# Cross attention scores: one float32r product of 96 stacked rows in place of a float32 product of 32 rows

## The chip, the cores and the metric

The program runs on one core of one Trainium2 chip. The metric is the device time of one execution in microseconds, the median of the runs shown. Lower is better. The core's engines are TensorE (PE, with its weight loads as PEld), VectorE (DVE), ScalarE (ACT), GpSimd (POOL) and SyncE (SP, which here only issues DMAs).

## The reference, cut to what matters

Six layers are applied to x (8 batches of 128 tokens, width 128) one after another, each with a residual: self attention, a cross attention to a context of 77 rows per batch, a mixture of 16 experts, a second self attention, the second cross attention, a mixture of 8 experts. The change touches only the two cross attentions:

```python
q = (query @ Wq + bq).reshape(B, Nq, H, D).transpose(0, 2, 1, 3)      # H = 16 heads, D = 8
k = (key_value @ Wk + bk).reshape(B, Nkv, H, D).transpose(0, 2, 1, 3) # Nkv = 77
v = (key_value @ Wv + bv).reshape(B, Nkv, H, D).transpose(0, 2, 1, 3)
attn = jnp.einsum('bhqd,bhkd->bhqk', q, k) * scale
attn = jnp.clip(attn, -CLAMP, CLAMP)          # the first cross attention only
attn = jax.nn.softmax(attn, axis=-1)
x = jnp.einsum('bhqk,bhkd->bqhd', attn, v).reshape(B, Nq, Cq)
return x @ Wo + bo
```

## The kernel before

The program is a row of blocks, written by hand, one instruction stream per engine, with semaphores between them; all engines meet between two blocks. In order: `setup_and_bias` (loads, keys and values of both cross attentions), `attention0` (the first self attention, four rounds; beside it GpSimd and SyncE prepare operands of later layers), a layer norm, `cross_attention(0)`, `mixture0`, `attention1`, a layer norm, `cross_attention(1)`, the rest of `mixture1`, `store`.

**Preparation beside attention0.** GpSimd makes `kblk` (L594): for each layer and batch a 128 x 308 tile, whose columns are 4 heads of a group times 77 keys. A row of head j holds the keys of that head in the columns of j and zeros elsewhere, so that one product of the 32 rows of a group of four heads gives the scores of all four. Behind that GpSimd splits the weights of 17 experts (L607, L609) that SyncE loads into two buffers (L584).

**cross_attention(l).** The queries of all 1024 tokens are two products of 512 columns (L666) that ScalarE moves to `q` with the bias (L740). Then there are 16 steps n, two for each batch; a step is 8 heads. In a step: the scores of two groups of four heads (L688, two products, in two banks of `x_score`); VectorE reads them (in layer 0 a clamp to `x_s`, L782, then the maximum, L799; in layer 1 the maximum, L785, then the subtraction, L803); GpSimd subtracts the maximum in layer 0 (L829); ScalarE takes the exponential (`x_p`, L769); TensorE transposes the 8 heads (`x_turn`, L722); ScalarE moves them to `x_pT` (L764); TensorE multiplies by the values (`x_pv`, L712). Once per batch the result is turned back (`x_back`, L732), normalized (L814, L818), turned again (L695) and multiplied by Wo (L680), added to x (L790), and the next layer norm is made (L795 to L837, L701).

TensorE's stream is software pipelined: in iteration n it issues the Wo product of an older batch, the scores of step n, the small turns, the values product of step n-2, the turn of step n-1 and the turn back. This order is fixed in the code:

```python
for u in range(2):
    at = 32 * (2 * (n % 2) + u)
    mm = pe.matmul(sbk[n % 2][:, u, 0:HG * NKV], q[at:at + 32, P * b:P * b + P],
                   kblk[l][at:at + 32, b, :], start=True, stop=True)
mm.then_inc(S["scores_done"], 1)
```

In layer 1 SyncE has one thing to do in this block: at its start it issues the first loads of the last mixture (`loads`); in layer 0 it has nothing.

Of the kernel before, what the change touches and what calls it, by code (L numbers as in the profile page):

```python
# [21 lines left out]
P = 128  # L22
B = 8
# [19 lines left out]
HG = 4  # L43
# [48 lines left out]
def program(nc, a, out, scratch, spread0):  # L92
# [30 lines left out]
    kblk = [sb(f"kblk{l}", [P, B, HG * NKV]) for l in range(2)]  # L123
# [98 lines left out]
    def setup_and_bias(bias0, w0):  # L222

        wq, wkv, wo = w0
        with ExitStack() as st:
            sb, ps, sem = tools(st, "su_")
# [107 lines left out]
    def attention0(bias0, w0):  # L334
# [3 lines left out]
        with ExitStack() as st:  # L338
# [15 lines left out]
            one = sb("one", [P, 1])  # L354
            fb = [ps(f"fill{j}") for j in range(2)]
# [5 lines left out]
                     "oT_dve", "y_done", "y_free", "kblk_done", "ld", "cast", "one_set", "landed0", "landed1")  # L361
            S = {n: sem(n) for n in names}
            block = st.enter_context(nc.Block())
# [210 lines left out]
            def _(sp):  # L574
# [6 lines left out]
                for e in range(E0 + 1):  # L581
                    if e >= 2:
                        sp.wait_ge(we_split, 2 * (e - 1))
                    sp.dma_start(raw[e % 2][:, :], a["experts0"][e].rearrange("p k m -> p (k m)")).then_inc(  # L584
                        S[f"landed{e % 2}"], 16)
                sp.wait_ge(S["ld"], 80)

            @block.gpsimd
            def _(pool):
                pool.memset(one[:, :], 1.0).then_inc(S["one_set"], 1)  # L590

                for l in range(2):
# [10 lines left out]
                pool.wait_ge(S["one_set"], 1)  # L603
# [7 lines left out]

    def cross_attention(l, loads=None):
# [3 lines left out]
        SLOTS = B + 2  # L616
        bo = (bo_x0, bo_x1)[l]
        with ExitStack() as st:
            sb, ps, sem = tools(st, f"x{l}_")
            q = sb("q", [P, T])  # L620
# [17 lines left out]
                     "xT_out", "pv_zeroed")  # L638
            if not xsem:
                xsem.update({n: gsem("x_" + n) for n in names})  # L640
            S = xsem
            one_layer = {"q_done": 2, "q_out": 2, "with_bias": 1, "pv_zeroed": 1, "slot_done": SLOTS}
            one_layer |= {n: STEPS for n in ("scores_done", "scores_read", "max_done", "shifted", "exp_done",
                                             "turn_done", "turned_out", "pv_done")}
            since = {n: l * one_layer.get(n, B) for n in names}
# [12 lines left out]
            if loads is not None:  # L658
# [1169 lines left out]
```

## Time and profile before

| | |
|---|---|
| median of 3 runs | 656.82 us (656.3, 656.82, 679.62) |
| span of the profiled execution (its own time beside the span isn't given) | 631.4 us |
| median less span | 25.4 us |
| busy in the span | PE 533.0, PEld 413.8, DVE 374.3, ACT 326.1, POOL 206.7 us |
| mean granted TensorE clock | 0.884 |
| window 190 to 262 us (cross attention 0) | PE 57.24 of 72 us, granted clock 0.83 |
| window 455 to 525 us (cross attention 1 from its scores on, and the start of mixture 1) | PE 60.66 of 70 us, granted clock 0.77 |
| the groups of L688 (scores) | 128 instructions, 28.5 us busy |

The table is read from the outside in: the span and the work around it make the time, the busy shares say which engine is nearest to the limit, and the windows say in which stage the changed lines lie. A share of busy time is no waiting time: which wait ends last in a step is seen only in the timeline of that step. The granted clock is the share of 2.4 GHz: 1.00 is 2.4 GHz and 0.50 is 1.2 GHz.

### The profile page before, as it was taken

Reading aid. Unit: us, or ns where it says so; the run is one execution under the profiler, and the core shown is the slowest. Engines: PE = TensorE matmul, PEld = TensorE weight load, DVE = VectorE, ACT = ScalarE, POOL = GpSimd, SP = SyncE. Lnnn points to the kernel's source line nnn. Section 1 sums busy time; section 2 is a strip of 40 time slices with the busy share of each in tenths; the row PEclk is TensorE's granted clock in tenths of the full one; section 3 lists DMA queues with packets and bytes.
Section 4 is the critical chain, followed back from the end, with each engine's and each line's share of the span. In section 5 each row is a group of like instructions: output and inputs, shape, how many; then the busy total and the mean of one; then the engine's idle time right before and its main releaser. Section 6 shows DMA issues by size and latency. Waiting matters only on the chain. (4 is left out here: it accounts for less than half of the span.)

```text
span 631.4 us, 9987 instructions
## 1 busy us (share of the span) xinstructions
PE 533.0 (84%) x3281; PEld 413.8 (66%) x3281; DVE 374.3 (59%) x875; ACT 326.1 (52%) x573; POOL 206.7 (33%) x229
## 2 busy tenths in 40 slices
PE   4698999989866998589999699864499967999996
PEld 2488898978853665457887387724266645777774
DVE  3376584756643465356666417765536638788875
ACT  3265454645403566435555326530246636788893
POOL 1688600000013346216655173011200255445510
PEclk9899999999876699789999569978559978899998
DMA  6913100000000000024432100000200001111201
GB/s 182 214 56 88 50 0 0 0 0 1 1 0 1 1 2 1 1 84 134 135 120 66 50 2 2 0 1 1 67 1 1 3 1 34 33 35 42 59 0 33
DMA packets 23412, 23.71 MB, mean 38 GB/s; under 512 B 3358, under 2 KB 17648, under 8 KB 23152
## 3 DMA queue, kind: packets, MB, share of 16 engines
q1 hardware_dynamic: 22528, 22.66, 12.5%
q10 hardware_dynamic: 848, 0.60, 0.3%
q8 instruction: 20, 0.33, 0.2%
q14 instruction: 16, 0.13, 0.1%
HBM read 22.64 MB, written 0.61 MB: 37 GB/s over the span
## 5 line engine op out<-in xcount | busy, mean ns | idle before, releaser
L1775 DVE TENSOR_TENSOR e_h_lo<-e_h,e_h_hi 128x512 fp32r<-128x512 f32 x60 | 50.7, 875 | 15.5 <-ACT e_h_hi L1636 15.4
L1045 POOL TENSOR_TENSOR e_gc<-e_g,e_c 128x512 f32<-128x512 f32 x32 | 42.0, 1314 | 42.0 <-ACT e_g L1028 22.4
L180 POOL TENSOR_TENSOR rstd<-var,eps_pow 128x4 f32<-128x4 f32 x8 | 8.3, 1039 | 134.0 <-DVE var L170 133.9
L722 PE MATMUL x_turn<-consts,x_p 128*77 128x128 f32 x256 | 42.3, 317 | 9.3 <-ACT x_p L769 9.3
L764 ACT ACTIVATE x_pT<-x_turn 77x1024 f32<-77x1024 f32 x32 | 32.6, 1020 | 32.9 <-PE x_turn L722 32.9
L1632 ACT ACTIVATE e_h<-e_h,m_b 128x512 f32<-128x512 f32 x64 | 43.6, 688 | 10.2 <-PE e_h L1534 10.2
L722 PEld LDWEIGHTS x_turn<-consts,x_p 128*77 128x77 f32 x256 | 33.7, 172 | 19.2 <-ACT x_p L769 16.4
L1093 DVE TENSOR_TENSOR e_h_lo<-e_h,e_h_hi 128x512 fp32r<-128x512 f32 x34 | 23.8, 699 | 26.0 <-ACT e_h_hi L1004 26.0
L1004 ACT ACTIVATE e_h_hi<-e_h 128x512 fp32r<-128x512 f32 x34 | 21.5, 632 | 33.9 <-DVE e_h L1087 28.2
L1636 ACT ACTIVATE e_h_hi<-e_h 128x512 fp32r<-128x512 f32 x64 | 38.6, 633 | 0.0
L416 PE MATMUL a_score<-a_kT,a_qz 128*128 128x128 f32 x256 | 34.5, 278 | 2.8 <-DMA rows<-in_L_xattn_bo 2.8
L416 PEld LDWEIGHTS a_score<-a_kT,a_qz 128*128 128x128 f32 x256 | 32.5, 192 | 4.2 <-issue 3.2
L444 PE MATMUL a_pv<-a_v,a_pT 128*128 128x65 f32 x256 | 33.6, 277 | 0.0
L485 ACT ACTIVATE a_qz<-a_fill 64x512 f32<-64x512 f32 x32 | 18.9, 591 | 28.1 <-PE a_fill L395 25.8
L444 PEld LDWEIGHTS a_pv<-a_v,a_pT 128*128 128x128 f32 x256 | 33.2, 201 | 0.3
L546 DVE SCALAR_TENSOR_TENSOR a_s<-a_score,w_bias 128x512 f32<-128x512 f32 x32 | 22.1, 690 | 18.0 <-PE a_score L416 17.7
L1674 POOL TENSOR_TENSOR m_w_hi<-m_w,e_one 128x512 fp32r<-128x512 f32 x16 | 17.5, 1096 | 44.7 <-PE e_y L1534 29.0
L829 POOL TENSOR_TENSOR x_s<-x_s,x_m 128x616 f32<-128x616 f32 x16 | 19.5, 1216 | 31.7 <-DVE x_m L799 31.7
L688 PE MATMUL x_score<-kblk,x_q 32*128 32x308 f32 x128 | 28.5, 561 | 1.6 <-ACT x_q L740 1.6
L515 ACT ACTIVATE a_p<-a_s 128x512 f32<-128x512 f32 x32 | 20.1, 629 | 18.2 <-DVE a_s L552 18.2
L782 DVE TENSOR_SCALAR x_s<-x_score 128x616 f32<-128x616 f32 x16 | 12.8, 799 | 27.2 <-PE x_score L688 26.7
L834 POOL TENSOR_TENSOR rstd<-var,eps_pow 128x1 f32<-128x1 f32 x16 | 9.0, 562 | 58.1 <-DVE var L809 58.1
(275 smaller groups left out, 1448.6 us busy)
## 6 DMA issues: line engine op xcount, KB each, us to landing
e_c<-spread SPq DMA_DIRECT2D x32, 256.0 KB, 3.2
m_w<-in_L_ffn_W SPq DMA_DIRECT2D x16, 256.0 KB, 3.0
a_raw<-in_experts SPq DMA_DIRECT2D x17, 192.0 KB, 2.4
su_reversed<-scratch SPq DMA_DIRECT2D x1, 1024.0 KB, 6.3
w_wkv<-in_L_attn_Wkv SPq DMA_DIRECT2D x1, 1024.0 KB, 8.7
a_pick_f<-in_pick SPq DMA_DIRECT2D x1, 768.0 KB
x_all<-in_x SPq DMA_DIRECT2D x1, 512.0 KB, 5.6
w_wq<-in_L_attn_Wq SPq DMA_DIRECT2D x1, 512.0 KB, 6.6
```

What stands on the lines that cost most here:

```text
L416: mm = pe.matmul(sbk[n % 2][:, h, :], qz[:, hg % 2, h, P * b:P * b + P], kT[:, hg % 2, h // 2, P * b:P * b + P], start=True, stop=True)
L444: mm = pe.matmul(ob[g % 2][:, h, 0:DH0 + 1], pT[g % 2][:, h, :], v[:, hg % 2, b, h, :], start=True, stop=True)
L546: dve.scalar_tensor_tensor(out=s[k][:, :, :], in0=sbk[k][:, :, :], scalar=SC, in1=bias0[:, NG * hg:NG * hg + NG, :], op0=ALU.mult, op1=ALU ...
L688: mm = pe.matmul(sbk[n % 2][:, u, 0:HG * NKV], q[at:at + 32, P * b:P * b + P], kblk[l][at:at + 32, b, :], start=True, stop=True)
L722: mm = pe.transpose(tb[0:NKV, u, P * j:P * j + P], p[k % 2][:, u, j, :], ident)
L764: act.activation(pT[k % 2][:, :, :], tb[0:NKV, :, :], ACT.Copy).then_inc(S["turned_out"], 1)
L1004: act.activation(h_hi[u % 2][:, :], h[u % 2][:, :], ACT.Copy).then_inc(S["hi_done"], 1)
L1045: pool.tensor_tensor(gc[k % 2][:, :], g[u % 2][:, :], c[k % NC][:, :], ALU.mult).then_inc(S["weighted"], 1)
L1093: dve.tensor_tensor(h_lo[u % 2][:, :], h[u % 2][:, :], h_hi[u % 2][:, :].bitcast(F32), ALU.subtract).then_inc(S["lo_done"], 1)
L1632: act.activation(h[half][f], hb[f][:, :], ACT.Gelu, bias=b1[j][:, f:f + 1]).then_inc(S["gelu_done"], 1)
L1636: act.activation(h_hi[half][f - 1][:, :], h[half][f - 1], ACT.Copy).then_inc(S["hi_done"], 1)
L1775: dve.tensor_tensor(h_lo[half][f][:, :], h[half][f], h_hi[half][f][:, :].bitcast(F32), ALU.subtract).then_inc(S["lo_done"], 1)
```

## The change

The scores are made of operands split in two float32r parts, high and low: q = q_hi + q_lo, k = k_hi + k_lo. Three of the four partial products are kept, stacked along the contraction: rows 0 to 31 hold q_hi against k_hi, rows 32 to 63 q_hi against k_lo, rows 64 to 95 q_lo against k_hi. So a group of four heads takes one float32r product of 96 rows and 308 columns in place of a float32 product of 32 rows.

The stacked keys (`kstack`) lie in DRAM, written beside `attention0`, and are loaded batch by batch into four buffers `ks`. The stacked queries `qs` are made in each cross attention by 24 copies from SBUF to SBUF, since each group's 32 rows must come to partitions 0, 32 and 64. The semaphores of `setup_and_bias` are cleared and freed at the start of `attention0` to have enough of them.

```diff
@@ attention0, GpSimd
-                    for b in range(B):
-                        pool.tensor_tensor(kblk[l][:, b, :].rearrange("p (h k) -> p h k", h=HG),
-                                           free(ctx_kT[l][:, b, :], [[0, HG], [1, NKV]]),
-                                           free(head_in_group, [[1, HG], [0, NKV]]),
-                                           ALU.mult).then_inc(S["kblk_done"], 1)
+                    whole = ctx_kT[l][:, :, :].rearrange("p b k -> p (b k)")
+                    if l == 1:
+                        pool.wait_ge(S["blk_lo_done"], B)
+                    pool.tensor_tensor(k_hi[:, :], whole, free(one[:, :], [[0, B * NKV]]), ALU.mult).then_inc(
+                        S["k_split"], 1)
+                    pool.wait_ge(S["k_split"], 2 * l + 1)
+                    pool.tensor_tensor(k_lo[:, :], whole, k_hi[:, :].bitcast(F32), ALU.subtract).then_inc(S["k_split"], 1)
+                    pool.wait_ge(S["k_split"], 2 * l + 2)
+                    if l == 1:
+                        pool.wait_ge(S["blk_stored"], 16 * 12)
+                    for which, (src, done) in enumerate(((k_hi, "blk_hi_done"), (k_lo, "blk_lo_done"))):
+                        for b in range(B):
+                            pool.tensor_tensor(blk[which][:, b, :].rearrange("p (h k) -> p h k", h=HG),
...
@@ attention0, SyncE: 24 stores to kstack between the loads of experts 1 and 2
+                def store_part(l, part, which):
+                    for g in range(4):
+                        sp.dma_start(kstack[l, :, 32 * part:32 * part + 32, g, :].rearrange("b r k -> r b k"),
+                                     blk[which][32 * g:32 * g + 32, :, :].bitcast(F32)).then_inc(S["blk_stored"], 16)
...
@@ cross_attention, SyncE
+                keys(0)
+                for j in range(2):
+                    half = slice(512 * j, 512 * j + 512)
+                    for pair in range(2):
+                        landed = S[f"qs_landed{2 * j + pair}"]
+                        for part, (src, out) in enumerate(((q_hi, "q_hi_out"), (q_hi, "q_hi_out"), (q_lo, "q_lo_out"))):
+                            sp.wait_ge(S[out], since[out] + j + 1)
+                            for g in (2 * pair, 2 * pair + 1):
+                                sp.dma_start(qs[32 * part:32 * part + 32, g, half].bitcast(F32),
+                                             src[32 * g:32 * g + 32, half].bitcast(F32)).then_inc(landed, 16)
+                    if j == 0:
+                        for b in range(1, KEYS):
+                            keys(b)
+                if loads is not None:
                     loads(sp)
+                for b in range(KEYS, B):
+                    sp.wait_ge(S["scores_done"], since["scores_done"] + 2 * (b - KEYS) + 2)
+                    keys(b)
@@ cross_attention, TensorE
+                        if n % 2 == 0:
+                            pe.wait_ge(S[f"ks_landed{b % KEYS}"], since[f"ks_landed{b % KEYS}"] + 16 * (b // KEYS + 1))
+                        if b % 4 == 0:
+                            landed = f"qs_landed{2 * (b // 4) + n % 2}"
+                            pe.wait_ge(S[landed], since[landed] + 16 * 6)
                         for u in range(2):
-                            at = 32 * (2 * (n % 2) + u)
-                            mm = pe.matmul(sbk[n % 2][:, u, 0:HG * NKV], q[at:at + 32, P * b:P * b + P],
-                                           kblk[l][at:at + 32, b, :], start=True, stop=True)
+                            g = 2 * (n % 2) + u
+                            mm = pe.matmul(sbk[n % 2][:, u, 0:HG * NKV], qs[:, g, P * b:P * b + P],
+                                           ks[b % KEYS][:, g, :], start=True, stop=True)
@@ cross_attention, ScalarE and VectorE
-                    act.activation(q[:, 512 * j:512 * j + 512], sbk[j][:, 0, :], ACT.Identity,
-                                   bias=cols[:, 3 * l:3 * l + 1]).then_inc(S["q_out"], 1)
+                    act.activation(q_hi[:, 512 * j:512 * j + 512], sbk[j][:, 0, :], ACT.Identity,
+                                   bias=cols[:, 3 * l:3 * l + 1]).then_inc(S["q_hi_out"], 1)
+                    dve.wait_ge(S["q_hi_out"], since["q_hi_out"] + j + 1)
+                    dve.scalar_tensor_tensor(out=q_lo[:, half], in0=sbk[j][:, 0, :], scalar=cols[:, 3 * l:3 * l + 1],
+                                             in1=q_hi[:, half].bitcast(F32), op0=ALU.add,
+                                             op1=ALU.subtract).then_inc(S["q_lo_out"], 1)
```

TensorE's order in the cross attentions stays as it was. The program before, from the query products to the fifth step of layer 0 (`x_score` are the two banks of scores, `x_turn` the transposed heads, `x_pv` the product with the values):

```order
L666 MATMUL x_score<-xnT_all,wqx 128x512 x2
L688 MATMUL x_score<-kblk,x_q 128x308 x4
L722 MATMUL x_turn<-consts,x_p 77x128 x8
L688 MATMUL x_score<-kblk,x_q 128x308 x2
L712 MATMUL x_pv<-x_pT,vx 9x128 x8
L722 MATMUL x_turn<-consts,x_p 77x128 x8
```

And the changed program at the same place:

```order
L727 MATMUL x_score<-xnT_all,wqx 128x512 x2
L755 MATMUL x_score<-x_ks,x_qs 128x308 x4
L789 MATMUL x_turn<-consts,x_p 77x128 x8
L755 MATMUL x_score<-x_ks,x_qs 128x308 x2
L779 MATMUL x_pv<-x_pT,vx 9x128 x8
L789 MATMUL x_turn<-consts,x_p 77x128 x8
```

The products stand where they stood, but the first four scores now read what SyncE has copied: the first two wait for six copies of queries and one load of keys, the next two for six more copies, and they stand ahead of the first turn. SyncE's queue in the changed program, in the block of cross attention 1 (`x_ks` stacked keys, `x_qs` stacked queries, `m_w` and `m_b` the weights of the last mixture):

```order
L703 DMA x_ks<-kstack 96x1232
L713 DMA x_qs<-x_q_hi 32x512 x4
L713 DMA x_qs<-x_q_lo 32x512 x2
L713 DMA x_qs<-x_q_hi 32x512 x4
L713 DMA x_qs<-x_q_lo 32x512 x2
L703 DMA x_ks<-kstack 96x1232 x3
L713 DMA x_qs<-x_q_hi 32x512 x4
L713 DMA x_qs<-x_q_lo 32x512 x2
L713 DMA x_qs<-x_q_hi 32x512 x4
L713 DMA x_qs<-x_q_lo 32x512 x2
L1554 DMA m_w<-in_L_ffn_W 128x512
```

Before, the loads of `m_w` and `m_b` were the whole queue of this block; they now stand behind 28 others. SyncE beside `attention0`, in the changed program, where before all 17 loads of `a_raw` stood in a row:

```order
L592 DMA a_raw<-in_experts 128x384 x2
L597 DMA kstack<-a_blk_hi 32x8x308 x8
L597 DMA kstack<-a_blk_lo 32x8x308 x4
L597 DMA kstack<-a_blk_hi 32x8x308 x8
L597 DMA kstack<-a_blk_lo 32x8x308 x4
L592 DMA a_raw<-in_experts 128x384 x15
```

Fifteen of the seventeen expert loads have moved behind the 24 stores.

## Rows read from the trace of the kernel before

**Rows 1.** Two stretches: us, busy PE, PEld, DVE, ACT, POOL, granted clock, DMA

```profile
209.00:213.00 4.00, 4.00 (x28) 2.34 (x28) 1.38 (x3) 1.85 (x3) 1.22 (x1) 0.50 0.00 0
...
252.00:256.00 4.00, 2.77 (x34) 2.10 (x32) 1.28 (x6) 1.95 (x4) 1.32 (x2) 1.00 0.00 0
```

**Rows 2.** Timeline, layer 0 at clock 0.50: start, us, engine, line, operation

```profile
206.19 1.40 PE L688 MATMUL x_score<-kblk,x_q 32*128 32x308 f32 x4
206.29 1.02 ACT L764 ACTIVATE x_pT<-x_turn 77x1024 f32<-77x1024 f32 x1 [2.59 <-PE x_turn L722]
207.51 1.04 PE L712 MATMUL x_pv<-x_pT,vx 77*9 77x128 f32 x16
```

**Rows 3.** Timeline, layer 1 at clock 1.00, one batch

```profile
484.53 1.02 ACT L764 ACTIVATE x_pT<-x_turn 77x1024 f32<-77x1024 f32 x1 [1.02 <-PE x_turn L722]
485.08 0.79 PE L688 MATMUL x_score<-kblk,x_q 32*128 32x308 f32 x4
485.45 0.70 ACT L769 ACTIVATE x_p<-x_s 128x616 f32<-128x616 f32 x1
485.80 0.62 PE L712 MATMUL x_pv<-x_pT,vx 77*9 77x128 f32 x16
...
486.36 1.10 PE L722 MATMUL x_turn<-consts,x_p 128*77 128x128 f32 x8
...
487.49 1.02 ACT L764 ACTIVATE x_pT<-x_turn 77x1024 f32<-77x1024 f32 x1 [0.40 <-PE x_turn L722]
...
488.56 0.62 PE L712 MATMUL x_pv<-x_pT,vx 77*9 77x128 f32 x16
```

**Rows 4.** Timeline, layer 0 at clock 1.00, one batch

```profile
221.39 0.79 PE L688 MATMUL x_score<-kblk,x_q 32*128 32x308 f32 x4
...
226.02 1.10 PE L722 MATMUL x_turn<-consts,x_p 128*77 128x128 f32 x8 [0.53 <-ACT x_p L769]
...
227.71 0.30 PEld L688 LDWEIGHTS x_score<-kblk,x_q 32*128 32x128 f32 x4
```

**Rows 5.** Chain that ended last: float32r products of 512 columns at both clocks

```profile
540.12 0.43 PE e_h L1533
...
543.31 0.23 PE e_h L1533
```

**Rows 6.** Timeline, the starts of both cross attentions

```profile
193.38 0.69 ACT L740 ACTIVATE x_q<-x_score,cols 128x512 f32<-128x512 f32 x1 [0.84 <-PE x_score L666]
...
195.49 0.80 PE L688 MATMUL x_score<-kblk,x_q 32*128 32x308 f32 x8 [0.78 <-ACT x_q L740]
...
200.05 1.99 PE L722 MATMUL x_turn<-consts,x_p 128*77 128x128 f32 x8 [3.76 <-ACT x_p L769]
...
451.23 0.69 ACT L740 ACTIVATE x_q<-x_score,cols 128x512 f32<-128x512 f32 x1 [0.84 <-PE x_score L666]
...
453.68 1.41 PE L688 MATMUL x_score<-kblk,x_q 32*128 32x308 f32 x8 [0.78 <-ACT x_q L740]
...
457.55 1.99 PE L722 MATMUL x_turn<-consts,x_p 128*77 128x128 f32 x8 [2.47 <-ACT x_p L769]
```

**Rows 7.** DMA issues: KB each, us from issue to landing (median)

```profile
spread<-e_wT SPq DMA_DIRECT2D x2, 32.0 KB, 2.3
```

**Rows 8.** Timeline, SyncE's queue: start and length of three issues

```profile
12.43 1.15 SPq L265 DMA_DIRECT2D wqx<-in_L_xattn_Wq  x1
...
19.23 0.43 SPq L270 DMA_DIRECT2D rows<-in_L_attn_gamma  x1
19.71 0.43 SPq L270 DMA_DIRECT2D rows<-in_L_attn_beta  x1
```

**Rows 9.** attention0: GpSimd's block tiles (group by line) and its last work (timeline)

```profile
L594 POOL TENSOR_TENSOR kblk<-ctx_kT,consts 128x308 f32<-128x308 f32 x16 | 10.6, 701 | 0.0
...
73.54 1.00 POOL L609 TENSOR_TENSOR we_lo<-a_raw,we_hi 128x384 fp32r<-128x384 f32 x1
```

**Rows 10.** VectorE's L552 in attention0: ns min/median/max of 32, first and last start

```profile
L552 DVE TENSOR_TENSOR a_s<-a_s,a_m x32: 691/692/1406, 32.1 to 168.9; 128x512 f32<-128x512 f32 x32
```

More of the change, by code:

```diff
@@ L89, in shape_constants, with program @@
     return np.ascontiguousarray(wide), hot, pick.reshape(CKV, E0 * P)
-def program(nc, a, out, scratch, spread0):
+def program(nc, a, out, scratch, spread0, kstack):
     ctx = ExitStack()
@@ L122, in program @@
     cols = sb("cols", [P, 16])
-    kblk = [sb(f"kblk{l}", [P, B, HG * NKV]) for l in range(2)]
     ctx_kT = [sb(f"ctx_kT{l}", [P, B, NKV]) for l in range(2)]
@@ L332, in _, with attention0 @@
                 norm_gpsimd(pool, 0)
-    def attention0(bias0, w0):
+        return mine
+    def attention0(bias0, w0, setup_sems):
         wq, wkv, wo = w0
@@ L354, in attention0 @@
             one = sb("one", [P, 1])
+            k_hi, k_lo = (sb(n, [P, B * NKV], F32R) for n in ("k_hi", "k_lo"))
+            blk = [sb(n, [P, B, HG * NKV], F32R) for n in ("blk_hi", "blk_lo")]
             fb = [ps(f"fill{j}") for j in range(2)]
@@ L619, in cross_attention @@
             sb, ps, sem = tools(st, f"x{l}_")
-            q = sb("q", [P, T])
+            q_hi, q_lo = (sb(n, [P, T], F32R) for n in ("q_hi", "q_lo"))
+            qs = sb("qs", [CKV, 4, T], F32R)
+            ks = [sb(f"ks{j}", [CKV, 4, HG * NKV], F32R) for j in range(KEYS)]
             s = [sb(f"s{j}", [P, 2, HG, NKV]) for j in range(2)]
@@ L637, in cross_attention @@
                      "y_done", "with_bias", "x_out", "stats_done", "aggr_done", "var_done", "rstd_done", "xn_done",
-                     "xT_out", "pv_zeroed")
+                     "xT_out", "pv_zeroed", "q_hi_out", "q_lo_out") + tuple(
+                         f"qs_landed{j}" for j in range(4)) + tuple(f"ks_landed{j}" for j in range(KEYS))
             if not xsem:
@@ L656, in scores, with _, keys @@
                 return sbk[n % 2][:, :, 0:HG * NKV].rearrange("p u (h k) -> p u h k", h=HG)
-            if loads is not None:
-                @block.sync
-                def _(sp):
+            @block.sync
+            def _(sp):
+                def keys(b):
+                    sp.dma_start(ks[b % KEYS][:, :, :].bitcast(F32), kstack[l, b]).then_inc(S[f"ks_landed{b % KEYS}"], 16)
+                keys(0)
[12 more added lines that the diff above has]
+                if loads is not None:
                     loads(sp)
+                for b in range(KEYS, B):
+                    sp.wait_ge(S["scores_done"], since["scores_done"] + 2 * (b - KEYS) + 2)
+                    keys(b)
             @block.tensor
@@ L774, in _ @@
                 dve.memset(ob[:, :], 0.0).then_inc(S["pv_zeroed"], 1)
+                for j in range(2):
+                    half = slice(512 * j, 512 * j + 512)
+                    dve.wait_ge(S["q_hi_out"], since["q_hi_out"] + j + 1)
+                    dve.scalar_tensor_tensor(out=q_lo[:, half], in0=sbk[j][:, 0, :], scalar=cols[:, 3 * l:3 * l + 1],
+                                             in1=q_hi[:, half].bitcast(F32), op0=ALU.add,
+                                             op1=ALU.subtract).then_inc(S["q_lo_out"], 1)
                 for n in range(2 * B + 8):
```

46 lines of the change are left out of this document (35 added, 11 removed).

## The prediction, made before the change was run

> **What bounds the kernel now.** I read the page first for the share of each engine and the clock, then the windows of the two cross attentions, then the timeline inside a step, because TensorE, busy most of the time there, need not be what ends last. At clock 0.50 (1.2 GHz) the windows show TensorE busy all the time [rows 1]. But the timeline shows what its work waits for [rows 2]: the pair of scores runs from 206.19 for 1.40 us, beside ScalarE's move of the turned heads, which runs from 206.29 to 207.31. The values product needs that move and begins at 207.51. So the scores lie under the move, except for the last 0.20 us. At 2.4 GHz in layer 1 it is the same [rows 3]: the move ends at 485.55, the scores at 485.87, the values product starts at 485.80, which is 0.25 after the move. In the batch's other step, where the scores came earlier, it starts 0.05 after the move (488.51 to 488.56). The scores thus hold it 0.20 back. The loop there is turn, move, exponential, turn. Only layer 0 at 2.4 GHz has the scores in its loop [rows 4]: scores at 221.39, clamp and maximum on VectorE, subtraction on GpSimd, exponential, turn at 226.02 (which waited 0.53 for ScalarE), turn back, Wo product, next scores at 227.71. The period is 6.32 us for a batch, and the scores' 0.79 is in it once.
>
> **What a pair of scores costs.** Before: 0.79 us at 2.4 GHz [rows 3, 4] and 1.40 at 1.2 [rows 2]. Twice the difference is what scales with the clock at 1.2 GHz, 1.22; the rest, 0.18, is fixed. The new products are float32r like those of the mixtures, where one of 512 columns takes 0.43 at 1.2 and 0.23 at 2.4 GHz [rows 5]. For 308 columns that is 0.26 and 0.14, for a pair 0.52 and 0.28. With the fixed 0.18 this makes 0.46 at 2.4 GHz and 0.70 at 1.2, if both weight loads are hidden. They hardly are, since the two products now share their rows of the array; I take 0.55 and 0.85. So a pair gains 0.25 at 2.4 GHz and 0.55 at 1.2; its bounds at 2.4 are 0.15 and 0.33.
>
> The rows and a rule speak against a larger gain. A pair is four instructions, two passes for each float32 product, and the group of L688 has 128 of them in 28.5 us of busy time, 0.22 each, though a pair alone scales with 0.61 at 2.4 GHz. The two products of a pair thus overlap. The Trainium skill, TensorE: Matmul & The Clock Gate, section "Part 3: Packing small matmuls — row/col tiling", says so: products of 32 rows at different row groups run concurrently, and a product of 32 rows takes no less time than one of 128. A product of 96 rows gives that up. Whoever counts the four instructions as one after another would put the gain at some 0.75 a pair, and the sum below by layer 0's five batches, some 2.5 us, lower.
>
> **The gain in the steps.** Low clock, four steps of each layer after the first turn: only the 0.20 behind the move is to be had, down to the usual 0.05, so 0.15 x 8 = 1.2 us. Layer 0 at 2.4 GHz: 0.25 for each of 5 batches, 1.25; late next is the loop of turn, move and exponential, which layer 1 shows to be shorter, so it doesn't stop the gain. Layer 1 at 2.4 GHz: the values product comes 0.20 earlier, but the turn behind it, at 486.36, then waits for the exponential, which ends at 486.15; 0.16 is left, and 6 batches make 1.0. Together 3.45 us.
>
> **The loss at the starts.** Before, the first scores follow the queries on ScalarE: in layer 0 these are done at 194.07 and the scores start at 195.49, the first turn at 200.05; in layer 1 451.92, 453.68 and 457.55 [rows 6]. Now SyncE waits for q_hi and issues six copies for the first two scores and six for the next two. VectorE's q_lo comes 0.7 after q_hi, while SyncE is still at the first four, and costs nothing. An issue takes 0.43 and the next follows at 0.48 [rows 8]. The nearest small transfer out of SBUF, 32 KB of 16 rows, lands 2.3 after its issue [rows 7]; I take that for a copy of 64 KB. The sixth copy is issued at 194.12 + 5 x 0.48 = 196.5 and lands at 198.8; the scores start at 198.95 and take 0.85 (the clock that was high at 195.49 won't be any more; the pair then took 0.80). The first turn comes 3.5 later, at 203.55. The second scores stand ahead of it in TensorE's order; their copies land at 201.7, so they don't hold it. In layer 1 the sixth copy lands at 456.7, so the first scores end at 457.6, against 455.09: 2.5 later. There the second scores decide: landed at 459.55, the turn right behind at 460.2, which is 2.65. Together 6.15 us. What else is queued behind these waits: the keys of batches 1 to 3 (needed from 203 on, issued by 201), the second half of the copies (needed a dozen us later), and in layer 1 the loads of the last mixture, which move some 15 us later and are used only after this block, over 40 us on. The bounds of the two starts together are 5 us (landing 0.5 us sooner) and, if each copy takes the 1.15 us of the slow issue in [rows 8], 19.
>
> A rule points the same way and further. The Trainium skill, DMA: Bandwidth & Descriptors, section "Rules for kernel authors", says to coalesce many small transfers, since under 64 KB one pays mostly overhead; its fixed cost is about 2.0 us a DMA. Against it the rows show issues that overlap at 0.48; if that cost came once for each copy, twelve of them would take 24 us and the sum would be some 30 us higher.
>
> **Beside attention0.** GpSimd had 16 tiles of 0.70 us and ended its work at 74.54 [rows 9], while this stage's last L552 starts at 168.9 [rows 10]. It gets 16 more tiles (11.2) and four passes of 616 columns (some 6), and waits for twelve stores in the middle; SyncE's loads of experts 2 to 16 stand behind all 24 stores. I put GpSimd's end at 100 to 120, which is hidden by some 50 us and more. What isn't hidden is that GpSimd and VectorE disturb each other: L552 takes 692 ns in the median and up to 1406 [rows 10]. 17 us more of such work reach over four steps, each with one L552; if each is 0.3 longer and half of that is seen, it is 0.6. I take +0.6, between 0 and 1.5. The clearing of the semaphores stands between two blocks: +0.1.
>
> **The clock.** In layer 0 it was still 0.50 at 213 us, 13 us after the first turn [rows 1, 6], and full at 221 [rows 4]; the turns back of the results join in between. In the changed kernel TensorE idles about 0.8 us in each low step, where it hardly did before; I take the rise relative to the first turn as it was, plus a little for where it falls in a step: +0.5, between -1 and +4. That it falls again in mid-layer is unlikely: at 252 to 256 TensorE was busy 2.77 of 4 us and the clock stayed 1.00 [rows 1].
>
> **The sum.** -3.45 + 6.15 + 0.6 + 0.1 + 0.5 = +3.9. The profiled span becomes 631.4 + 3.9 = 635.3, and with the 25.4 us between span and median 660.7. That is 0.6% slower, no change as a measurement goes: of this kernel it can tell some 2%, 13 us, from nothing (one of its three runs is 23 us above the others).
>
> **Rivals.** (1) The clock stays at 1.2 GHz for longer, since the scores gave TensorE work that is now missing. For it: it didn't rise in 13 us although TensorE was busy for 4.00 of 4 us [rows 1]. Against it: the full work around the turns back is still there. A batch at 1.2 GHz is two steps of turn 1.99, move 1.02 and values 1.04 [rows 2, 6], 8.1 to 8.3 us, where it is 6.0 now (twice 487.49 - 484.53 in [rows 3]), 2.2 more; from four late batches of the twelve on it is over 2%, and if it never rises the time is 687. (2) The copies go slowly: at 1.15 us each the starts cost 13 more, 674; at 0.8, 667. (3) The scores are on the path everywhere, since the releasers in the rows are only inferred: 24 steps at 0.25 and 8 at 0.55 give 10.4 in place of 3.45, and 653.7. Against it: where the scores came early, the values product began 0.05 behind the move, as it must if the move is what it waits for [rows 3]. (4) The stores and the loads behind them run so slowly that attention0 waits for GpSimd: that needs stores of 315 KB at 60 GB/s or less, where 32 KB landed in 2.3 us [rows 7], and gives 680 or more. (5) The product isn't done as float32r and costs what it did: 664.
>
> **How the numbers follow.** Forecast 0.62; (1) 0.13, of which 0.08 above 2%; (2) 0.08, of which 0.03; (3) 0.12; (4) 0.03; (5) 0.02. The forecast's own range is 657 to 665, its terms' bounds together. The range goes from 654 (most of rival 3) to 670 and leaves out 0.14 above and some 0.04 below. Faster by over 2% needs 13 us, more than all terms of rival 3: 0.02. Slower by over 2%: 0.08 + 0.03 + 0.03 = 0.14. Within: 0.84.
>
> **What would show it.** In the changed profile: pairs of x_score at 0.5 to 0.6 us at 2.4 GHz; first turns 9.5 and 8.3 us after the end of the first query move (6.0 and 5.6 in [rows 6]); the period in layer 0 at 6.05; the values product 0.05 behind every move; GpSimd idle before 125. I am wrong if the copies are issued at over 0.7 us apart, if the clock rises later than 18 us after the first turn, or if x_pv starts 0.05 behind the move and the period still doesn't shrink.

## The result and the profile after

The changed kernel took 633.5 us in the median of 4 runs (631.72, 633.9, 638.12, 633.09), the kernel before 656.91 (656.3, 656.82, 679.62, 657.0). The ratio is 0.966, interval 0.961 to 0.970: 23 us faster, where I had forecast 4 us slower.

The page of the changed kernel: span, busy time of each engine, granted clock in 40 slices.

```profile
span 630.0 us, 9992 instructions
PE 515.5 (82%) x3217; PEld 409.3 (65%) x3217; DVE 378.9 (60%) x879; ACT 326.3 (52%) x573; POOL 224.8 (36%) x249
PEclk9899999999876799689999569978569978899998
```

The span is only 1.4 us below the 631.4 of before. So the gain is not between these two traces. What gives it away is the time around the span: the changed kernel's runs list their spans too, and the difference is 1.7 to 1.8 us in each (631.72 and 630.0 in the profiled one), where I had taken 25.4. If before has the same difference, its traced execution was one of some 633 us, and not one of those at 657 that its median stands for. The next section tests this.

Stretches of both cross attentions after the change (columns as in [rows 1]):

```profile
204.00:214.00 10.00, 8.76 (x59) 6.29 (x58) 4.34 (x7) 4.66 (x6) 3.65 (x3) 0.52 1.00 243
214.00:252.00 38.00, 31.98 (x384) 24.08 (x384) 24.20 (x58) 27.10 (x43) 21.22 (x22) 1.00 0.12 33
450.00:466.00 16.00, 8.43 (x41) 5.52 (x40) 6.30 (x8) 3.42 (x5) 0.00 (x0) 0.50 0.66 159
467.00:507.00 40.00, 34.26 (x426) 25.89 (x426) 26.12 (x62) 28.76 (x46) 6.82 (x10) 1.00 0.32 83
```

Its timeline: the starts of both cross attentions (these answer to [rows 6]), two turns at 1.2 GHz, and a batch of layer 0 at 2.4 GHz (answers to [rows 4]). SPq rows are SyncE's issues.

```profile
192.62 2.50 SPq L713 DMA_DIRECT2D x_qs<-x_q_hi  x4
...
197.95 0.85 PE L755 MATMUL x_score<-x_ks,x_qs 96*128 96x308 f32 x2 [4.49 <-DMA x_qs<-x_q_lo]
...
202.44 0.88 PE L755 MATMUL x_score<-x_ks,x_qs 96*128 96x308 f32 x2 [3.63 <-DMA x_qs<-x_q_lo]
...
203.12 1.91 PE L789 MATMUL x_turn<-consts,x_p 128*77 128x128 f32 x8
...
207.19 1.99 PE L789 MATMUL x_turn<-consts,x_p 128*77 128x128 f32 x8
...
211.26 1.14 PE L789 MATMUL x_turn<-consts,x_p 128*77 128x128 f32 x4
...
220.60 1.10 PE L789 MATMUL x_turn<-consts,x_p 128*77 128x128 f32 x8
...
222.11 0.53 PE L755 MATMUL x_score<-x_ks,x_qs 96*128 96x308 f32 x2
...
226.47 1.10 PE L789 MATMUL x_turn<-consts,x_p 128*77 128x128 f32 x8 [0.23 <-ACT x_p L836]
...
449.70 0.69 ACT L807 ACTIVATE x_q_hi<-x_score,cols 128x512 fp32r<-128x512 f32 x1 [0.84 <-PE x_score L727]
...
455.66 0.85 PE L755 MATMUL x_score<-x_ks,x_qs 96*128 96x308 f32 x2 [4.29 <-DMA x_qs<-x_q_lo]
...
460.02 1.91 PE L789 MATMUL x_turn<-consts,x_p 128*77 128x128 f32 x8
```

The reader is to see: a pair of scores now takes 0.85 us at 1.2 GHz and 0.53 at 2.4; a batch of layer 0 takes 5.87 us at 2.4 GHz (from the turn at 220.60 to that at 226.47) and took 6.32; and the first scores wait 4.5 and 4.3 us for copies.

The clock of layer 1 before, in the traced execution, for the comparison further down:

```profile
452.00:474.00 22.00, 18.75 (x110) 11.13 (x108) 7.90 (x10) 8.50 (x11) 0.00 (x0) 0.50 0.09 25
475.00:511.00 36.00, 33.86 (x381) 23.30 (x381) 23.39 (x60) 24.98 (x42) 7.94 (x12) 1.00 0.01 2
```

### The profile page after: what moved, and what is told of

It reads as the page before. It is cut to its first block and busy times, and to the rows that moved or that the text cites. A ratio compares the mean times of both kernels' runs of the same rounds, so it can differ in the third digit from the quotient of the medians.

```text
span 630.0 us, 9992 instructions
## 1 busy us (share of the span) xinstructions
PE 515.5 (82%) x3217; PEld 409.3 (65%) x3217; DVE 378.9 (60%) x879; ACT 326.3 (52%) x573; POOL 224.8 (36%) x249
## 5 line engine op out<-in xcount | busy, mean ns | idle before, releaser
L1848 DVE TENSOR_TENSOR e_h_lo<-e_h,e_h_hi 128x512 fp32r<-128x512 f32 x60 | 49.1, 846 | 16.5 <-ACT e_h_hi L1709 16.4
L789 PE MATMUL x_turn<-consts,x_p 128*77 128x128 f32 x256 | 39.5, 303 | 1.2 <-ACT x_p L836 1.2
L1166 DVE TENSOR_TENSOR e_h_lo<-e_h,e_h_hi 128x512 fp32r<-128x512 f32 x34 | 23.8, 699 | 26.1 <-ACT e_h_hi L1077 26.1
L789 PEld LDWEIGHTS x_turn<-consts,x_p 128*77 128x77 f32 x256 | 31.8, 163 | 9.8 <-ACT x_p L836 9.3
L755 PE MATMUL x_score<-x_ks,x_qs 96*128 96x308 f32 x64 | 19.8, 396 | 16.1 <-DMA x_qs<-x_q_lo 15.2
L836 ACT ACTIVATE x_p<-x_s 128x616 f32<-128x616 f32 x32 | 22.6, 707 | 14.7 <-POOL x_s L902 7.8
L779 PE MATMUL x_pv<-x_pT,vx 77*9 77x128 f32 x512 | 21.2, 287 | 10.2 <-ACT x_pT L831 10.2
```

Of the source, the lines that this page charges most:

```text
L789: mm = pe.transpose(tb[0:NKV, u, P * j:P * j + P], p[k % 2][:, u, j, :], ident)
L1166: dve.tensor_tensor(h_lo[u % 2][:, :], h[u % 2][:, :], h_hi[u % 2][:, :].bitcast(F32), ALU.subtract).then_inc(S["lo_done"], 1)
L1848: dve.tensor_tensor(h_lo[half][f][:, :], h[half][f], h_hi[half][f][:, :].bitcast(F32), ALU.subtract).then_inc(S["lo_done"], 1)
```

## The experiments

### Where the 24 us lie: the kernel before again

> The kernel before, unchanged, to see where its 25.4 us between span and median lie. Theory A (clock): its time is its span plus about 1.75 us, as in all four runs of the changed kernel, and the spans differ among executions: some at 631 us (the profiled one), most at 655, some at 678, and the mean granted clock falls with them (0.884, then about 0.85 and 0.82), because in one or two stages TensorE stays at 1.2 GHz some 40 to 80 us longer. Theory B (outside the span): spans of 631 us beside times of 656, a difference of 25 us in each run.

Measured: 682.26, 628.33, 627.24, 634.21, 676.8, 657.9; the profiled one is the 682.26, and its span is 680.5. So the time lies in the span: time less span is 1.7 to 1.9 us in every execution of before that lists both. Its page and three stretches:

```profile
span 680.5 us, 9987 instructions
...
PEclk9699999999755555689998779795555556799999
```

```profile
186.00:271.00 85.00, 79.04 (x464) 49.87 (x464) 33.35 (x74) 33.73 (x50) 28.36 (x28) 0.50 0.00 1
459.00:575.00 116.00, 97.35 (x553) 63.87 (x554) 48.93 (x135) 43.34 (x70) 25.12 (x30) 0.50 0.04 10
500.00:512.00 12.00, 12.00 (x83) 7.56 (x82) 5.28 (x10) 5.03 (x9) 0.00 (x0) 0.50 0.01 1
```

Both cross attentions ran at 1.2 GHz from end to end. The last row is the surprise: TensorE was busy for 12.00 of 12 us, and the clock stayed down. One batch there, TensorE's rows:

```profile
511.73 1.99 PE L722 MATMUL x_turn<-consts,x_p 128*77 128x128 f32 x8
513.52 1.06 PE L732 MATMUL x_back<-consts,x_oS 128*128 128x128 f32 x4
514.37 0.63 PE L680 MATMUL x_score<-wox,x_oT 128*128 128x128 f32 x2
514.93 1.40 PE L688 MATMUL x_score<-kblk,x_q 32*128 32x308 f32 x4
516.26 1.04 PE L712 MATMUL x_pv<-x_pT,vx 77*9 77x128 f32 x16
517.23 1.99 PE L722 MATMUL x_turn<-consts,x_p 128*77 128x128 f32 x8
...
522.07 1.99 PE L722 MATMUL x_turn<-consts,x_p 128*77 128x128 f32 x8
```

No row is idle before its work (the other pair of scores, 1.40 too, lies where rows are left out): the batch is 10.3 us of TensorE's own work, where a batch of layer 1 at 2.4 GHz took 6.0. The last Wo product of each block gives the price of a whole cross attention:

```profile
279.08 0.79 PE L680 MATMUL x_score<-wox,x_oT 128*128 128x128 f32 x2 [0.37 <-ACT x_oT L749]
...
561.26 0.79 PE L680 MATMUL x_score<-wox,x_oT 128*128 128x128 f32 x2 [0.37 <-ACT x_oT L749]
```

The query products began at 189.92 and 470.84, so the two blocks took 89.2 and 90.4 us up to there. In the first trace of before it was 66.5 (191.30 to 257.82) and 64.1 (449.14 to 513.25). That is 22.6 and 26.3 more, together nearly all of the 49.1 us between the two spans.

Over all the runs shown here and below, the kernel before was executed 54 times, its first trace not counted: 6 took 627 to 635 us, 39 took 651 to 663, 9 took 673 to 683. Where the mean granted clock is listed it goes with the group: 0.884 to 0.891, 0.829 to 0.854, 0.794 to 0.812. I read each step of some 24 us as one cross attention in which the clock doesn't rise; traces show executions with none (the first trace), one (next run) and two (this one) such.

### The cleared semaphores

> The kernel before with one thing of the change: the semaphores of the setup are allocated by hand and cleared and freed at the start of attention0. Theory A (clock): this does nothing, 656 us with spans near 655. Theory B (something outside the span is cheaper since the change): 633 us. My prediction's term for it was +0.1 us.

```diff
+                mine.append(nc.alloc_semaphore(f"su_{name}"))
...
+            nc.clear_and_free_semaphores(setup_sems)
```

Measured: 656.38 us median (651.72 to 658.73) beside 655.15. The 24 us don't come from here. Its profiled execution (654.17, span 652.4) shows the common case, in which one layer rises and the other doesn't:

```profile
212.00:256.00 44.00, 37.05 (x410) 24.95 (x408) 25.64 (x68) 27.73 (x46) 22.35 (x25) 1.00 0.01 2
434.00:526.00 92.00, 79.07 (x464) 49.85 (x464) 39.71 (x106) 33.85 (x50) 11.31 (x13) 0.50 0.04 12
```

### The product alone

> The kernel before with kblk and q written as float32r, so that the scores are float32r products of 32 rows; it leaves out the low parts of queries and keys. No copies, no stores, no splitting, nothing starts later. If the cheaper product itself is what makes the clock rise sooner or more surely: 625 to 632 us. If the later start, the copies or the other parts of the change do it, and the product brings only the path's 3.5 us: 652 us. If TensorE needs fuller rows of its array for the clock, and 32 rows in float32r are less work than before: 656 us or more, up to 680.

> As e3_rows32, but each product takes rows 0 to 95 of q and kblk, whatever is in them: the scores come from three groups at once and the low parts are left out. It is the changed kernel's product (float32r, 96 rows, 308 columns) without its copies, stores and later starts. If the product alone makes the 23 us: 625 to 630 us (the starts' 6 us are not paid). If the number of rows decides and not the cheaper product, this one is near 627 and e3_rows32 at 650 or more. If the later starts or the stores do it: 652 us, like e3_rows32.

```diff
-    kblk = [sb(f"kblk{l}", [P, B, HG * NKV]) for l in range(2)]
+    kblk = [sb(f"kblk{l}", [P, B, HG * NKV], F32R) for l in range(2)]
...
-            q = sb("q", [P, T])
+            q = sb("q", [P, T], F32R)
...
 e4 also:
-  ... q[at:at + 32, P * b:P * b + P], kblk[l][at:at + 32, b, :] ...
+  ... q[0:96, P * b:P * b + P], kblk[l][0:96, b, :] ...
```

Measured: 627.81 (622.68 to 633.56) and 621.78 (618.55 to 627.42), beside 655.15. By their times, the clock rose in both layers in all 12 executions. So the cheaper product alone is enough, with nothing else of the change. That 96 rows come out 6 us lower than 32 was not expected; the two profiled executions differ by only 0.8 us (626.4 and 625.6), and what makes the rest isn't settled.

### Freed time, or the kind of product?

Two causes were left: the time that cheaper scores free at 1.2 GHz (theory A1), or float32r itself (theory A2).

> As e3_rows32 (float32r products of 32 rows, low parts left out), but each pair of scores is issued twice, the second over the first: the same result, and TensorE has about as much to do as in the kernel before (some 1.3 us a pair at 1.2 GHz in place of 1.40). Theory A1, the time that the cheaper scores free makes the clock rise: it rises as unreliably as before, median near 655, executions at 630, 655 and 680. Theory A2, the kind of product decides, float32r in place of float32: the clock rises in both cross attentions in every execution, and the time is e3_rows32's 628 plus at most the doubled pairs, 628 to 636.

> The kernel before, float32, with only the first of the two score products of each step; the other bank is set to zero once, so the scores of half the heads are left out. TensorE's time for a step's scores falls by a good third, as with float32r, but its kind stays. Theory A1 (the freed time decides): clock rises in both, all executions at 622 to 634. Theory A2 (float32r itself decides): median 650 or more, with executions some 24 us apart.

Measured: e5 632.94 (624.61 to 634.14), e6 656.52 (652.74 to 664.35), beside 655.62. That looked like A2. But e6's timeline shows that it had freed nothing:

```profile
488.77 1.39 PE L688 MATMUL x_score<-kblk,x_q 32*128 32x308 f32 x2
```

One product of 32 rows takes 1.39 us where two at once take 1.40. And in e5 the pair, issued twice over, still took only 0.88 us. So both runs fit A1 as well. The next two tell them apart: one holds the time and changes the kind, the other changes the time and holds the kind.

> e6_half freed no time of TensorE (one float32 product took 1.39 us at 1.2 GHz, two at once 1.40), and e5_twice still freed some 0.5 us a pair, so the two theories are still apart. Here the pair of float32r products (32 rows, low parts left out) is issued four times over itself: 0.62 + 3 x 0.26 = 1.40 us at 1.2 GHz, exactly the time of the float32 pair. Theory A1 (freed time makes the clock rise): as before, median 650 or more with executions 24 us apart. Theory A2 (the kind of product does): the clock rises in both cross attentions in every execution, and the time is 629 to 638, since at 2.4 GHz the four cost about 0.1 more than the float32 pair.

> The kernel before, float32, but each score product has 154 of its 308 columns, so that the pair takes about 0.7 us at 1.2 GHz in place of 1.40: time is freed as with float32r, and the kind of product stays. It leaves out the scores of half the heads. Theory A1 (freed time): the clock rises in both, all executions at 622 to 634. Theory A2 (kind of product): the clock stays at 1.2 GHz through cross attention 1 in most executions, each batch 8.5 us there in place of 10.2, median 638 to 648.

```diff
 e5 (float32r, the pair issued twice)
+                        for twice in range(2):
+                            for u in range(2):
...
 e6 (float32, one product)
-                        for u in range(2):
+                        for u in range(1):
 e10 (float32r, the pair issued four times)
+                        for again in range(4):
+                            for u in range(2):
...
 e11 (float32, half the columns)
-  sbk[n % 2][:, u, 0:HG * NKV] ... kblk[l][at:at + 32, b, :]
+  sbk[n % 2][:, u, 0:HALF_C]   ... kblk[l][at:at + 32, b, 0:HALF_C]
```

e6 and e11 also set the second half of each score tile to zero at the start of the block; e6, which gained nothing, shows that this is not what helps.

TensorE's rows of a step at 1.2 GHz in e10, then in e11, and a later stretch of e11:

```profile
473.55 1.39 PE L689 MATMUL x_score<-kblk,x_q 32*128 32x308 f32 x8
474.87 1.04 PE L713 MATMUL x_pv<-x_pT,vx 77*9 77x128 f32 x16
```

```profile
465.92 0.88 PE L689 MATMUL x_score<-kblk,x_q 32*128 32x154 f32 x4
467.10 1.04 PE L713 MATMUL x_pv<-x_pT,vx 77*9 77x128 f32 x16 [0.30 <-ACT x_pT L765]
```

```profile
480.00:514.00 34.00, 29.35 (x344) 21.02 (x343) 21.92 (x62) 21.89 (x39) 9.30 (x14) 1.00 0.01 2
```

Measured: e10 637.74, 660.54, 677.4, 657.97, 628.26, 635.68; e11 632.0 (629.32 to 637.43, ratio 0.965, interval 0.961 to 0.969). With float32r and no freed time, three executions of six are 24 or 48 us up again. With float32 and 0.52 us freed in each pair, none of six is; e5 and e11, with 0.88 us a pair in either kind, come to 632.9 and 632.0. A2 falls: float32r isn't needed. That e10 did better than before (3 of 6 executions near 630 against 6 of 54) leaves room for a smaller part of the kind of product; this stays open.

What "freed time" does is open too. In e11's rows above TensorE is idle only 0.30 us before one product. Shorter scores also move the steps: its first turn in layer 1 comes 7.9 us after the query products began, where it was 8.4 before. Idle time and shifted steps were not separated here.

### The late start

> The kernel before with its scores unchanged, and a late start alone: TensorE waits, before the first scores of each cross attention, for two small copies of queries, one after the other, which starts them some 4 us later, as in the changed kernel. Theory A1 (the time that cheaper scores free at 1.2 GHz): nothing gained, median 655 + 8 = 660 to 666. Theory H3 (the late start shifts the steps against whatever the clock looks at, and that makes it rise): clock high in both, 632 to 640.

```diff
+            @block.sync
+            def _(sp):
+                sp.wait_ge(S["q_out"], since["q_out"] + 1)
+                for i in range(2):
+                    sp.dma_start(idle[:, 512 * i:512 * i + 128], q[:, 0:128]).then_inc(S["late"], 16)
+                    sp.wait_ge(S["late"], since["late"] + 16 * (i + 1))
...
 TensorE:
+                pe.wait_ge(S["late"], since["late"] + 32)
```

Measured: 661.04, 632.85, 634.66, 633.12, 632.24, 636.6, 632.38, beside 655.73. The kernel before gains some 23 us from a wait. The wait is 2 us and not the 4 that I had written: in its trace of layer 1 the first scores, at 481.05, start 6.5 us after the query products began (before: 4.5). They cost what they did:

```profile
481.05 1.41 PE L694 MATMUL x_score<-kblk,x_q 32*128 32x308 f32 x8 [2.71 <-issue]
```

```profile
200.00:290.00 90.00, 84.01 (x519) 56.05 (x517) 30.96 (x76) 35.58 (x58) 27.73 (x31) 0.50 0.00 1
```

My expectation under A1 alone, 660 to 666, was wrong, and H3's range holds. The last row is layer 0 of the same execution, the 661, in which the clock missed the rise there. So a late start makes the rise in both layers likely, but not sure: 6 executions of 7. The change brings both causes at once, and each is enough for most of the gain by itself.

### The changed kernel again, and its copies

> The changed kernel, unchanged, for how surely its clock rises and for comparison on the same chip. Theory A1: every execution between 629 and 640, none near 655 or 680. If its four executions so far were luck: one or two of six near 655.

Measured: 628.92 (627.31 to 633.46) beside 655.73. With the first four runs that is ten executions, all between 627 and 639. Had its chance of missing a rise been that of before (48 of 54), this would not be seen.

> The changed kernel, with the copies of queries for the first four batches shared between two queues: SyncE issues those of groups 0 and 2, ScalarE those of groups 1 and 3, behind its moves of the queries. If the issue of one queue (0.62 us a copy) holds the starts: the first scores start 1.9 us sooner in each layer, the first turn 2 to 3.5 sooner, 627 to 630. If the landing of the copies or the DMA engines hold them: 632 to 635. If the sooner start costs the clock its early rise, as the traces before and after would allow (it rose 14.7 us after the first turn before, 10.8 after): no gain, 632 or more.

```diff
+                for pair in range(2):
+                    copies(act, 0, pair, (2 * pair + 1,))
```

Measured: 634.2 (628.8 to 636.02) beside 656.63, no gain over the changed kernel's 633.5 and 628.92. The issues are done sooner, the last landings hardly. The two ACTq rows are the last issues for the first and for the second scores:

```profile
191.33 0.60 ACTq L705 DMA_DIRECT2D x_qs<-x_q_lo  x1
...
193.26 0.61 ACTq L705 DMA_DIRECT2D x_qs<-x_q_lo  x1
...
193.52 0.85 PE L758 MATMUL x_score<-x_ks,x_qs 96*128 96x308 f32 x2 [3.51 <-DMA x_qs<-x_q_lo]
...
198.61 0.88 PE L758 MATMUL x_score<-x_ks,x_qs 96*128 96x308 f32 x2 [4.24 <-DMA x_qs<-x_q_lo]
```

Counted from the query products (186.26 here, 189.82 in the changed kernel), the first scores start 7.3 us later in place of 8.1, the second 12.4 in place of 12.6. The second wait until 4.7 us after the end of the last issue that they need (193.87). SyncE had meanwhile issued the keys of three batches, 462 KB each, which take 4.3 us to land in this trace; that they hold up the copies is likely, not shown. Something else took from the gain: in this trace the clock of layer 1 rose at 474, 28.6 us after the query products began, and in both traces of the changed kernel (with e17) after less than 19. From the first query product to the last Wo product that block took 66.1 us here and 63.3 and 63.4 there.

> The same arithmetic as the changed kernel (high and low parts, three of four products), but as three float32r products of 32 rows for each group, added up in the bank, the two groups of a step in turn. No copies of queries; the low keys of a layer come in two loads. The first scores start 4.5 us after the query products as in the kernel before, where the changed kernel starts them at 8.1. If the starts cost what I predicted (6.15 us for the two) and the three passes take 0.6 to 0.8 us a pair: 626 to 631. If three passes of 32 rows take as much of TensorE's time as float32 did and that is what keeps the clock low: 650 or more. If the late start itself helps the clock to rise and is worth its wait: 633 or more.

```diff
+                        three = ((q_hi, kb_hi[l]), (q_hi, kb_lo), (q_lo, kb_hi[l]))
+                        for i, (qq, kk) in enumerate(three):
+                            for u in range(2):
+                                at = 32 * (2 * (n % 2) + u)
+                                mm = pe.matmul(sbk[n % 2][:, u, 0:HG * NKV], qq[at:at + 32, P * b:P * b + P],
+                                               kk[at:at + 32, b, :], start=i == 0, stop=i == 2)
```

Measured: 632.95 (630.11 to 638.1) beside 655.62. The same precision without copies comes to the same time, not to the 626 to 631 that the earlier start alone would give. Two things stand against the start: dearer scores (at 1.2 GHz the six products begin at 210.14 and end at 211.28, 1.14 us where the stacked pair takes 0.85), and, in this trace, a late rise of the clock in layer 0. How much each takes isn't separated.

```profile
210.14 0.62 PE L720 MATMUL x_score<-kb_hi,x_q_hi 32*128 32x308 f32 x2
...
210.82 0.46 PE L720 MATMUL x_score<-kb_hi,x_q_lo 32*128 32x308 f32 x2
```

```profile
200.00:233.00 33.00, 32.80 (x231) 24.19 (x232) 12.52 (x22) 13.51 (x20) 9.51 (x9) 0.50 0.01 2
234.00:252.00 18.00, 16.16 (x201) 12.03 (x201) 12.27 (x30) 11.97 (x21) 9.87 (x11) 1.00 0.01 1
```

Here the clock did rise, 44 us after the query products began (189.81), with TensorE busy for 32.80 of the 33 us before. So idle time in the steps can't be all that a late rise needs.

### Filler: the rise on purpose

> The changed kernel with filler: 16 float32r products of 512 columns behind the query products and 6 behind the first scores, written to the bank of turned heads that nobody reads yet. They stand where TensorE waits anyway (7.4 us for copies, then 4.3 us for the exponential); nothing of the result changes. If dense work of TensorE ahead of the steps brings the clock to 2.4 GHz: it is at 1.00 by the first turn in both layers, the four steps at 1.2 GHz shrink from 4.1 to 2.9 us each, and the time falls by 5 to 10 us to 623 to 629. If filler does nothing for the clock: 633 to 636.

> The kernel before with filler alone: 6 float32r products of 512 columns behind the query products and 5 behind the first scores, into the bank of turned heads. The scores stay float32. If the clock only needs a start (once at 2.4 GHz the float32 steps keep it, as the trace before shows from 221 us on): it is high in both layers in every execution, 622 to 632. If float32 steps at the low clock can't raise it and the filler's rise is lost before the first turn: as before, median 655.

```diff
+                def fill(count):
+                    for _ in range(count):
+                        pe.matmul(tb[:, 0, :], we_hi[:, 0, 0, :], we_hi[:, 0:2, :, :].rearrange(
+                            "p e k m -> p (e k m)")[:, 0:512], start=True, stop=True)
...
 behind the query products:
+                fill(6)
...
 behind the scores of step 0:
+                        if n == 0:
+                            fill(5)
...
 e8 has 16 and 6, e16 16 and 12, both on the changed kernel; e14 is e13 with
+                        if n == 1 and l == 0:
+                            fill(6)
```

Measured: e8 630.93 (629.11 to 632.87) beside 655.62; e13 626.7 (625.14 to 630.25) beside 656.63, ratio 0.957, interval 0.954 to 0.960. Eleven products whose result nobody reads, in each cross attention, do at least as much as the change does: its ratio is 0.966, and 0.959 when run again (e17). e8 missed its 623 to 629: filler on the changed kernel gives next to nothing. In e13 layer 1 runs at 2.4 GHz from 450 us on, but layer 0 rose and fell again:

```profile
187.00:194.00 7.00, 5.29 (x24) 3.08 (x23) 3.19 (x4) 1.52 (x3) 1.50 (x2) 0.98 0.00 0
194.00:218.00 24.00, 24.00 (x156) 15.44 (x154) 8.43 (x12) 9.98 (x14) 7.00 (x6) 0.50 0.00 1
...
450.00:504.00 54.00, 49.02 (x519) 32.52 (x518) 33.31 (x76) 33.29 (x54) 8.61 (x13) 1.00 0.02 5
```

> e13_before_fill (the kernel before with filler, float32 scores) with 6 more filler products behind the second scores of layer 0. In the trace of e13_before_fill the clock of layer 0 had risen at 187.4 and fell at 194.2, after a wait of 1.71 us for the first exponential, and came back only at 218.1. If filler in that wait keeps the clock: layer 0 runs its steps at 2.4 GHz from the first turn on, some 10 us less than that trace, and 617 to 623. If the waits between the next steps bring it down all the same: 625 to 629.

> e8_fill (the changed kernel with filler) with 12 filler products behind the first scores in place of 6; in its trace of layer 0 the clock fell after waits of 1.76 and 1.06 us. If that holds the clock: 622 to 628. If the waits for the keys of batch 1 still break it: 629 to 633 as e8_fill.

Measured: e16 630.73 (628.15 to 633.77); e14 620.66 (618.6 to 623.91), both beside 655.73 and, on the same chip, 628.92 for the changed kernel. e16 missed its 622 to 628: in its trace the clock rose early in both layers, fell again (at 209 and 465) and was back 4 us later. With six more fillers in layer 0 both layers of e14 are at 2.4 GHz before the first turn, and stay there. It is the best of the kernels with full precision: 0.947 of before, 8 us below the changed one, and its six executions lie within 5.3 us.

```profile
197.27 1.10 PE L732 MATMUL x_turn<-consts,x_p 128*77 128x128 f32 x8
```

```profile
193.00:250.00 57.00, 49.31 (x520) 32.63 (x518) 33.22 (x76) 33.98 (x54) 27.72 (x29) 1.00 0.01 1
445.00:499.00 54.00, 49.03 (x519) 32.52 (x518) 33.29 (x76) 33.29 (x54) 8.62 (x13) 1.00 0.02 4
```

## Why the prediction was wrong

**The step that failed** is in the sum: "The profiled span becomes 631.4 + 3.9 = 635.3, and with the 25.4 us between span and median 660.7." I took 25.4 us as work around the span. They are 1.75; the other 24 are a cross attention at 1.2 GHz (23 to 26 us, e1) in most executions of before, which the traced one didn't have. No row showed work around the span; the term was a difference between a median and another execution's span, and I gave it to both kernels alike. The 679.62 among the three runs was a hint: it is 23 us above the others, the same distance again. I mentioned it as noise only.

**The rivals** had the right mechanism with the wrong sign: (1) let the clock stay low for longer after the change and gave it 0.13. That it was the kernel before that mostly stayed low, and the change could cure it, I didn't list. Its price was too small as well: 2.2 us a batch, from the first steps only; with the turns back and the Wo product a batch at 1.2 GHz is 10.3 (e1), so 4.3.

**Against executions of the same kind there is next to no difference.** Before's six executions with both rises have a median of 629.2 (627.24 to 634.21), the changed kernel's ten 631.7 (627.31 to 638.12). The two ranges overlap and come from several chips, so neither the 2.5 us nor its sign is shown. In the two first traces the cross attentions, from the first query product to the last Wo product, took 66.5 and 64.1 us before, 66.7 and 63.3 after: 0.6 less together, where my terms for them gave 3.2 more. In the changed kernel's second trace (e17) it is 69.2 and 63.4, 2.0 more. The terms:

- Pair of scores: 0.55 and 0.85 predicted, 0.53 and 0.85 measured.
- Low-clock steps: 0.15 less predicted; 4.07 now (203.12, 207.19, 211.26) and 4.22 before, as said.
- Layer 0 at 2.4 GHz: period 6.05 predicted, 5.87 measured. The gain is 0.45 a batch, 1.7 times what a pair gains (0.26); I had the scores in that loop once. That they are in it nearly twice is my reading, untested.
- The starts: first turns 9.5 and 8.3 us after the end of the first query move predicted. Measured 10.5 (192.60 to 203.12) and 9.6 (450.39 to 460.02), 8.5 us more in all, not 6.15. An issue takes 0.62 and not 0.48, a copy of 64 KB lands after 3.1 us (median) and not 2.3. The working of layer 1 had a slip besides: scores that land at 459.55 and take 0.85 end at 460.4, not 460.2.
- The clock, +0.5: wrong sign in these traces. In layer 1 it is at 1.00 from 467 on, 7 us after the first turn; in the traced execution of before it was 0.50 until 474, over 16 us after it. In layer 0 it is high by 214, 11 us after the first turn, against 14.7. With the cheaper scores this gave back the starts: in layer 1 the first turn comes 4.0 us later and the block is 0.8 shorter. In e17 the clock of layer 0 rose 30 us after the query products began, in place of 24, and the block was 2.5 us longer.
- Beside attention0: GpSimd ended its splitting at 105.9, inside 100 to 120, and the cross attention began at 189.8 against 191.3: the +0.6 isn't seen. Semaphores: no effect seen (e2), where I had 0.1.

**What is shown and what isn't.** Shown: a cross attention of before in which the clock stays at 1.2 GHz costs 23 to 26 us more, and by time and granted clock this happens in one or both of them in 48 of 54 executions; shorter scores (e11, e3) or a start 2 us later (e15) cure nearly all of it, each alone, and filler cures it too. Not shown: which of the two acts in the changed kernel, since it has both, and why a rise depends on 2 us. One thing more stands in the traces. In the kernels with float32 scores at full cost and no filler (before, e1, e2, e6, e15), the clock of a cross attention either rose 23 to 25 us after the query products began (five times) or not at all (five times). In kernels with cheaper scores it also rose after 28 to 34 us (e3, e5, e11, e12, e17), in e7's layer 0 after 44. That cheaper scores give the clock such a second chance is argued, not shown, and it doesn't hang on idle time alone: e7's late rise came with TensorE packed, and so did one of e10's, after 33 us.

## What to carry to other kernels

Before adding "the rest of the time" to a span, look at whether the traced execution is a typical one: equal distances between the times of single runs (629, 655 and 679 us here) hint that a stage runs in one of two ways, and a stage's price at the other clock belongs in the sum. A stage that starts out of a pause at 1.2 GHz with TensorE packed can stay there to its end (e1); products that nobody reads, put where TensorE waits anyway, brought the clock up and were worth more than the rewriting of the scores (e14), but added nothing to it (e16). An edit that shifts such a stage by 2 us can move the time by 23, so test the shift alone before crediting the edit.

## What the hardware showed that I had not expected

- A granted clock of 0.50 for 85 us (e1) and for 92 (e2), with TensorE busy 79 us of each and 12.00 of 12 in mid-stage (e1): the clock stayed down all the same.
- One float32 product of 32 rows and 308 columns took 1.39 us at 1.2 GHz, and two in different rows of the array 1.40: leaving one out saves nothing.
- Sharing twelve small copies between two queues cut the issue and hardly the wait: the last of them landed 4.7 us after its issue, with 1.4 MB of keys issued meanwhile (e12).
